# Two attention stages: GpSimd's jobs between the masks, the two turns on TensorE exchanged, a row's sum one place later

## The chip, the cores and the metric

The kernel runs on one core of a Trainium2 chip, in one launch. The time is device microseconds from start to end of one execution. Three executions of the kernel before took 1243.11, 1254.38 and 1258.14 us; their median, 1254.38 us, is the time before.

## The reference

x has 8 rows of 512 tokens of 128 features. Two layers follow each other. Each adds to x an attention and a feed-forward part, both computed from the normalized x:

```python
xn = _layernorm(x)
x = x + _L0_attn_ref(xn, ...) + _L0_ffn_ref(xn, ...)   # amplitude and phase attention; attention over 8 batches, experts (top 1)
xn = _layernorm(x)
x = x + _L1_attn_ref(xn, ...) + _L1_ffn_ref(xn, ...)   # plain attention with biases; experts (top 2)
```

The attention of both layers, which is what the change touches, is causal softmax attention with 16 heads of 8 features over each row of 512 tokens, and a projection by Wo:

```python
scores = where(mask, q @ k.T / sqrt(8), -inf)          # layer 0: of (cos, sin) pairs, scaled for each head
attn = softmax(scores)
out = (attn @ v) @ Wo.T
```

## The kernel before, in words

The program is a list of stages that don't overlap; two of them, `attend0` and `attend1`, are the function `attend` (line 1915) for layer 0 and layer 1. A unit is 4 heads (a group, `GH` = 4) of one row; there are 8 rows of 4 groups, so 32 units. All of a unit's data are f16 stacks of q and k that SyncE loads from HBM into a ring of four places.

Each engine has its own queue, written out by hand as a sequence of steps (`all_steps`, line 164, unrolled). In step t the engines work on several units at once. For unit t, TensorE computes all scores in five chunks c0 to c4 (`maxima`) into a ring of two pairs of PSUM banks, and VectorE reduces each chunk to negated maxima (`reduce`; c1 and c3 in two instructions). For unit t-1 the maxima are split into two f16 parts (`split_maxima`, VectorE), turned by TensorE (`turn_maxima`, one product with 32 columns of weights), copied out of PSUM (`copy_maxima`), and sent by SyncE into two rows of the q tile. For unit t-2 TensorE computes the shifted scores again, transposed, in five chunks and two sides (`probabilities`), with one PSUM bank for each side, ScalarE exponentiates each (`exponentials`) and GpSimd zeroes the upper triangles of the diagonal blocks (`mask`, four for each unit). For unit t-3 TensorE multiplies by the values in four pieces (`mix`: mix 0 behind c1, mix 1 behind c2, mix 2 and 3 behind c3; f32, four heads side by side in column tiles of 32), and ScalarE copies the result to SBUF (`mixT`). For unit t-4 TensorE turns that copy (`turn_mix`, four square f32 transposes) and VectorE divides by the sums (`divide`). Where t-4 is the last group of a row, the step also has `turn_context` (four square transposes, behind c2), a copy by ScalarE, `project` (behind c4), and VectorE's sum of the row (`add_row`).

The three turns and the projection share one PSUM bank, `TURN`, which sets much of the order. In the kernel before, `turn_mix(t-4)` stands behind c0 (line 2233) and `divide` behind the reduction of c0; `turn_maxima(t-1)` stands behind c1 and mix 0 (line 2240), waits for `divide` to have emptied the bank (line 2220), and `copy_maxima` follows the reduction of c1. `add_row(t-4)` is the last thing in VectorE's step (line 2328), before the next step's `split_maxima`; the next `turn_mix` waits for it (line 2216).

GpSimd's queue (lines 2073 to 2093) goes unit by unit: copy the values of unit n into a ring of two (line 2078), start one gather of 128 rows by an indirect DMA in layer 0 or two in layer 1 (line 2086), the four masks of unit n, and in layer 1 two additions for unit n-1 that join the gathered experts' results into `x_sum` (`join_branches`, line 2052). GpSimd's unit n coincides with the step n+2 of the other engines. In layer 0 the gathered rows are used only in a later stage.

## Time and profile before

| | |
|---|---|
| time, median of 3 runs | 1254.38 us (1243.11 to 1258.14) |
| time of the profiled execution | 1254.72 us |
| its span, first to last instruction | 1253.1 us, mean granted clock 0.889 |
| `attend0`, first to last copy of the maxima | 401.6 us to 634.5 us |
| `attend1`, first load of q to the end | 975.7 us to 1253.1 us |

The profile is of one execution. PE is TensorE's matmuls and PEld its weight loads, DVE is VectorE, ACT is ScalarE, POOL is GpSimd; L2171 is line 2171 of the listing. In brackets behind a row of the timeline stands how long the engine had been idle and what ended that. The ends of matmuls are modelled, their starts and those of weight loads are recorded, so pieces of work on TensorE are best measured from weight load to weight load.

### The profile page before, as it was taken

Reading aid. Unit: us, or ns where it says so; the run is one execution under the profiler, and the core shown is the slowest. Engines: PE = TensorE matmul, PEld = TensorE weight load, DVE = VectorE, ACT = ScalarE, POOL = GpSimd, SP = SyncE. Lnnn points to the kernel's source line nnn. Section 1 sums busy time; section 2 is a strip of 40 time slices with the busy share of each in tenths; the row PEclk is TensorE's granted clock in tenths of the full one; section 3 lists DMA queues with packets and bytes.
Section 4 is the critical chain, followed back from the end, with each engine's and each line's share of the span. In section 5 each row is a group of like instructions: output and inputs, shape, how many; then the busy total and the mean of one; then the engine's idle time right before and its main releaser. Section 6 shows DMA issues by size and latency. Waiting matters only on the chain. (4 is left out here: it accounts for less than half of the span.)

```text
span 1253.1 us, 25971 instructions
## 1 busy us (share of the span) xinstructions
PE 996.1 (79%) x8908; PEld 650.2 (52%) x8908; DVE 832.1 (66%) x1875; ACT 680.5 (54%) x1293; POOL 586.7 (47%) x862
## 2 busy tenths in 40 slices
PE   3789753989874999999976463499999699999997
PEld 1456531777672455555533332388888345555542
DVE  1566331799986899999927666133333799999992
ACT  1266443776720777777755353122222377777774
POOL 3467537244432444455433466111110477777774
PEclk9899766899996899999997575699999599999998
DMA  4322032477775222222202233466664111112110
GB/s 135 110 49 54 27 100 89 139 206 201 217 156 132 70 70 70 70 73 77 61 7 63 76 106 96 146 183 192 190 184 136 43 45 53 53 53 53 53 47 27
DMA packets 151525, 122.57 MB, mean 98 GB/s; under 512 B 31712, under 2 KB 134032, under 8 KB 151408
## 3 DMA queue, kind: packets, MB, share of 16 engines
q1 hardware_dynamic: 141664, 102.89, 29.6%
q0 software_dynamic: 8016, 17.71, 4.9%
q8 instruction: 67, 1.10, 0.4%
q10 hardware_dynamic: 1728, 0.46, 0.2%
q14 instruction: 50, 0.41, 0.1%
HBM read 75.75 MB, written 42.61 MB: 94 GB/s over the span
## 5 line engine op out<-in xcount | busy, mean ns | idle before, releaser
L2103 ACT ACTIVATE attend_probs<-attend_attend_ps 128x512 f32<-128x512 f32 x640 | 353.7, 600 | 152.7 <-PE attend_attend_ps L2171 141.5
L2171 PE MATMUL attend_attend_ps<-attend_q,attend_ks 50*128 50x512 f16 (+3 forms) x1024 | 236.6, 307 | 23.1 <-ACT attend_probs L2103 20.3
L2070 POOL TENSOR_SCALAR_AFFINE_SELECT attend_probs<-attend_probs 128x512 f32<-128x512 f32 x256 | 159.6, 636 | 196.7 <-ACT attend_probs L2103 196.1
L2139 PE MATMUL attend_attend_ps<-attend_ks,attend_q 48*128 48x512 f16 (+3 forms) x1024 | 191.5, 317 | 27.8 <-DMA attend_ks<-k_stack 20.2
L2184 PE MATMUL attend_attend_ps<-attend_probs,attend_vals 128*32 128x512 f32 (+3 forms) x2048 | 183.2, 455 | 0.0
L2266 DVE TENSOR_REDUCE attend_neg_max<-attend_attend_ps 128x2 f32<-128x1024 f32 x128 | 155.5, 1215 | 14.3 <-PE attend_attend_ps L2151 9.0
L2151 PE MATMUL attend_attend_ps<-identb,stairs 64*128 64x128 bf16 (+1 forms) x1280 | 144.5, 213 | 0.0
L2171 PEld LDWEIGHTS attend_attend_ps<-attend_q,attend_ks 50*128 50x128 f16 x1024 | 70.4, 94 | 121.6 <-ACT attend_probs L2103 73.7
L2268 DVE TENSOR_REDUCE attend_neg_max<-attend_attend_ps 128x2 f32<-128x768 f32 x128 | 121.9, 952 | 8.2 <-PE attend_attend_ps L2151 7.3
L2151 PEld LDWEIGHTS attend_attend_ps<-identb,stairs 64*128 64x128 bf16 x1280 | 104.4, 100 | 19.3 <-issue 4.7
L1886 PE MATMUL experts_experts_ps<-experts_rowsT,experts_w_in 128*128 128x256 f32 (+1 forms) x468 | 110.2, 386 | 1.6 <-ACT experts_rowsT L1835 1.5
L1851 DVE TENSOR_TENSOR experts_hidden<-experts_experts_ps,experts_gate 128x512 f32<-128x512 f32 x39 | 27.0, 691 | 120.3 <-ACT experts_gate L1827 120.3
L1091 POOL DMA_INDIRECT sorted<-middle_scaled,rank_row x64 | 65.6, 1025 | 59.7 <-issue 39.3
L1814 POOL DMA_DIRECT2D experts_rows<-sorted x39 | 27.7, 711 | 136.7 <-issue 136.7
L1886 PEld LDWEIGHTS experts_experts_ps<-experts_rowsT,experts_w_in 128*128 128x128 f32 (+1 forms) x468 | 82.5, 183 | 17.7 <-ACT experts_rowsT L1835 2.1
L2139 PEld LDWEIGHTS attend_attend_ps<-attend_ks,attend_q 48*128 48x128 f16 x1024 | 68.3, 96 | 41.5 <-DMA attend_ks<-k_stack 20.6
L1827 ACT ACTIVATE experts_gate<-experts_experts_ps 128x512 f32<-128x512 f32 x39 | 23.3, 597 | 121.0 <-PE experts_experts_ps L1886 121.0
L2263 DVE TENSOR_REDUCE attend_neg_max<-attend_attend_ps 128x4 f32<-128x1024 f32 x64 | 78.4, 1225 | 9.6 <-PE attend_attend_ps L2151 9.2
L2086 POOL DMA_INDIRECT attend_moe<-done,back_row x64 | 62.1, 970 | 15.1 <-issue 15.1
L1898 PE MATMUL experts_experts_ps<-experts_w_out,experts_hidden 128*128 128x128 f32 (+1 forms) x468 | 58.7, 275 | 0.9 <-DVE experts_result L1862 0.9
L2184 PEld LDWEIGHTS attend_attend_ps<-attend_probs,attend_vals 128*32 128x32 f32 x2048 | 45.3, 110 | 26.9 <-issue 9.5
L1898 PEld LDWEIGHTS experts_experts_ps<-experts_w_out,experts_hidden 128*128 128x128 f32 (+1 forms) x468 | 55.4, 191 | 1.2 <-issue 1.1
(316 smaller groups left out, 1933.4 us busy)
## 6 DMA issues: line engine op xcount, KB each, us to landing
experts_w_in<-in_L_ffn_w_dram SPq DMA_DIRECT2D x78, 176.0 KB, 2.4
q_stack<-middle_parts SPq DMA_DIRECT2D x24, 256.0 KB
k_stack<-middle_parts SPq DMA_DIRECT2D x24, 256.0 KB
attend_q<-q_stack SPq DMA_DIRECT2D x64, 96.0 KB
attend_ks<-k_stack SPq DMA_DIRECT2D x64, 96.0 KB
middle_w_in<-in_L_ffn_W_dram SPq DMA_DIRECT2D x23, 256.0 KB
middle_w_out<-in_L_ffn_W_dram SPq DMA_DIRECT2D x23, 256.0 KB
experts_rows<-sorted POOLq DMA_DIRECT2D x39, 128.0 KB, 2.5
```

The source lines that it names most:

```text
L1091: pool.indirect_dma_start(k.sorted1, bass.IndirectOffsetOnAxis(ap=k.rank_row[:, c * NT + tile:c * NT + tile + 1], axis=0), scaled[:, c, ti ...
L1886: mm = pe.matmul(ps[0:size[c], hidden_bank(u, bank), half * ROWS:(half + 1) * ROWS], w_in[:, u.phase, w + c * P:w + c * P + size[c]], rows ...
L1898: mm = pe.matmul(ps[:, OUT, a * D:(a + 1) * D], hidden[0:size[c], u.par, c, a * P:(a + 1) * P], w_out[0:size[c], u.phase, c, :], start=(c ...
L2070: pool.affine_select(out=block_, in_=block_, compare_op=ALU.is_ge, fill=0.0, base=0, pattern=[[0, GH], [1, P]], channel_multiplier=-1).the ...
L2103: act.activation(probs[:, u.par, 2 * c + side, :], ps[:, PROB + side, :], ACT.Exp, scale=SCALE ** -2)\
L2139: pe.matmul(ps[:, bank + side, col:col + (qt + 1) * P], q[rows(side, KR), g, pair, qt * P:(qt + 1) * P], ks[rows(side, KR), g, pair, 0:(qt ...
L2151: mm = pe.matmul(span[:, :, col:col + 64], k.stairs[here, stair:stair + P], k.identb[here, here].unsqueeze(1).broadcast_to([64, len(blocks ...
L2171: mm = pe.matmul(ps[:, PROB + side, col:col + S - kt * P], ks[rows(side, KM), g, pair, kt * P:(kt + 1) * P], q[rows(side, KM), g, pair, kt ...
L2184: mm = pe.matmul(ps[32 * h:32 * h + 32, MIX, kt * P:S], vals[:, u.par, kt * GH + h, :], probs[:, u.par, 2 * c + h % 2, col:col + S - kt * ...
L2263: ins = dve.tensor_reduce(out[:, :, :, 1], pair_banks.rearrange("p s (h t) -> p s h t", h=HP), X_AXIS, ALU.max, negate=True)
L2266: ins = dve.tensor_reduce(out[:, :, c // 2, 3], pair_banks, X_AXIS, ALU.max, negate=True)
L2268: dve.tensor_reduce(out[:, :, c // 2, 2], pair_banks[:, :, 0:384], X_AXIS, ALU.max, negate=True)
```

## The change

It touches only `attend`, so both stages, and is a change of order with the waits that belong to it. No arithmetic instruction, DMA or buffer is added or taken away.

1. GpSimd: `copy_values(0)` comes first; then for each unit n: mask 0, the gather (0), in layer 1 the join of branch 0 of unit n-1, masks 1 to 3, the copy of the values of unit n+1, and in layer 1 the second gather and the join of branch 1 of unit n-1. The joins of the last unit stand behind the loop.
2. TensorE: `turn_maxima(t-1)` moves from behind c1 and mix 0 to behind c0; `turn_mix(t-4)` moves from behind c0 to behind c1 and mix 0. The waits for the bank are exchanged: the turn of the maxima waits for the division of unit t-5 and, after a row's end, for the row's sum; the turn of the mix waits for the copy of the maxima of unit t-1.
3. VectorE: `copy_maxima` follows the reduction of c0, `divide` that of c1. `add_row` leaves the end of step t and stands in step t+1 behind `split_maxima`.

```diff
@@ -2049,14 +2049,29 @@
                     pool.wait_ge(k.z_out[i].sem, (TILES[0] + Z_RING - 1 - i) // Z_RING * 16)
             src, at_row = ((k.done0, k.rank_row[:, NT:2 * NT]), (k.done1, k.back_row[:, :]))[layer]
 
-            def join_branches(n):
-
-                for c in range(2):
-                    m = 2 * n + c
-                    pool.wait_ge(gathered[m % 4].sem, (m // 4 + 1) * 16)
-                    if c:
-                        pool.wait_ge(joined.sem, joined.after(n, 0))
-                    pool.tensor_tensor(k.x_sum[:, n, :], k.x_sum[:, n, :], moe[:, c * NT + n, :], ALU.add).then_inc(joined.sem, 1)
+            def copy_values(n):
+                if n >= 2:
+                    pool.wait_ge(mixed.sem, mixed.done(n - 2))
+                b, g = divmod(n, NG)
+                pool.tensor_copy(vals[:, n % 2, :, 0:HD].rearrange("p (j h) d -> p j h d", j=QT),
+                                 k.v_all[:, b, :, g * GH * HD:(g + 1) * GH * HD].rearrange("p j (h d) -> p j h d", h=GH))\
+                    .then_inc(vals_ready.sem, 1)
+
+            def gather(n, c):
+                m = n * (layer + 1) + c
+                if m >= 4:
+                    pool.wait_ge(gathered[m % 4].sem, m // 4 * 16)
+                pool.indirect_dma_start(moe[:, c * NT + n, :], None, src,
+                                        bass.IndirectOffsetOnAxis(ap=at_row[:, c * NT + n:c * NT + n + 1], axis=0))\
+                    .then_inc(gathered[m % 4].sem, 16)
+
+            def join_branch(n, c):
+
+                m = 2 * n + c
+                pool.wait_ge(gathered[m % 4].sem, (m // 4 + 1) * 16)
+                if c:
+                    pool.wait_ge(joined.sem, joined.after(n, 0))
+                pool.tensor_tensor(k.x_sum[:, n, :], k.x_sum[:, n, :], moe[:, c * NT + n, :], ALU.add).then_inc(joined.sem, 1)
 
             def mask(n, i):
 
@@ -2070,27 +2085,25 @@
                 pool.affine_select(out=block_, in_=block_, compare_op=ALU.is_ge, fill=0.0, base=0,
                                    pattern=[[0, GH], [1, P]], channel_multiplier=-1).then_inc(masked.sem, 1)
 
-            for n in range(UNITS + JOIN_AFTER * layer):
-                if n < UNITS:
-                    if n >= 2:
-                        pool.wait_ge(mixed.sem, mixed.done(n - 2))
-                    b, g = divmod(n, NG)
-                    pool.tensor_copy(vals[:, n % 2, :, 0:HD].rearrange("p (j h) d -> p j h d", j=QT),
-                                     k.v_all[:, b, :, g * GH * HD:(g + 1) * GH * HD].rearrange("p j (h d) -> p j h d", h=GH))\
-                        .then_inc(vals_ready.sem, 1)
-
-                    for c in range(layer + 1):
-                        m = n * (layer + 1) + c
-                        if m >= 4:
-                            pool.wait_ge(gathered[m % 4].sem, m // 4 * 16)
-                        pool.indirect_dma_start(moe[:, c * NT + n, :], None, src,
-                                                bass.IndirectOffsetOnAxis(ap=at_row[:, c * NT + n:c * NT + n + 1], axis=0))\
-                            .then_inc(gathered[m % 4].sem, 16)
-                if n < UNITS:
-                    for i in range(QT):
-                        mask(n, i)
+
+            copy_values(0)
+            for n in range(UNITS):
+                mask(n, 0)
+                gather(n, 0)
                 if layer == 1 and n >= JOIN_AFTER:
-                    join_branches(n - JOIN_AFTER)
+                    join_branch(n - JOIN_AFTER, 0)
+                for i in range(1, QT):
+                    mask(n, i)
+                if n + 1 < UNITS:
+                    copy_values(n + 1)
+                if layer == 1:
+                    gather(n, 1)
+                    if n >= JOIN_AFTER:
+                        join_branch(n - JOIN_AFTER, 1)
+            if layer == 1:
+                for n in range(UNITS - JOIN_AFTER, UNITS):
+                    for c in range(2):
+                        join_branch(n, c)
             for i in range(4):
                 pool.wait_ge(gathered[i].sem, UNITS * (layer + 1) // 4 * 16)
 
@@ -2207,19 +2220,17 @@
 
 
 
+            def before_maxima(t):
+                if active(t, 5, UNITS):
+                    pe.wait_ge(context_done.sem, context_done.done(t - 5))
+                    if (t - 5).group == NG - 1:
+                        pe.wait_ge(added.sem, added.done((t - 5).row))
+
             def before_mix(t):
-                if active(t, 2, UNITS):
-                    pe.wait_ge(maxT_ready.sem, maxT_ready.done(t - 2))
-                elif active(t, 5, UNITS):
-                    pe.wait_ge(context_done.sem, context_done.done(t - 5))
-                if active(t, 5, UNITS) and (t - 5).group == NG - 1:
-                    pe.wait_ge(added.sem, added.done((t - 5).row))
-
-            def before_maxima(t):
-                if active(t, 4, UNITS):
-                    pe.wait_ge(context_done.sem, context_done.done(t - 4))
-                elif active(t, 2, UNITS):
-                    pe.wait_ge(maxT_ready.sem, maxT_ready.done(t - 2))
+                if active(t, 1, UNITS):
+                    pe.wait_ge(maxT_ready.sem, maxT_ready.done(t - 1))
+                else:
+                    before_maxima(t)
 
             def step(t):
                 row_ends = active(t, 4, UNITS) and (t - 4).group == NG - 1
@@ -2230,19 +2241,17 @@
                         maxima(t, c)
                     if active(t, 2, UNITS):
                         probabilities(t - 2, c, 1)
-                    if c == 0 and active(t, 4, UNITS):
-                        before_mix(t)
-                        turn_mix(t - 4)
+                    if c == 0 and active(t, 1, UNITS):
+                        before_maxima(t)
+                        turn_maxima(t - 1)
                     if 1 <= c <= 3 and active(t, 3, UNITS):
                         mix(t - 3, c - 1)
                         if c == 3:
                             mix(t - 3, 3)
-                    if c == 1 and active(t, 1, UNITS):
-                        before_maxima(t)
-                        turn_maxima(t - 1)
+                    if c == 1 and active(t, 4, UNITS):
+                        before_mix(t)
+                        turn_mix(t - 4)
                     if c == 2 and row_ends:
-                        if active(t, 1, UNITS):
-                            pe.wait_ge(maxT_ready.sem, maxT_ready.done(t - 1))
                         turn_context(t - 4)
                     if c == 4 and row_ends:
                         project(t - 4)
@@ -2318,15 +2327,15 @@
             def step(t):
                 if active(t, 1, UNITS):
                     split_maxima(t - 1)
+                if active(t, 5, UNITS) and (t - 5).group == NG - 1:
+                    add_row(t - 5)
                 for c in range(MCH):
                     if active(t, 0, UNITS):
                         reduce(t, c)
-                    if c == 0 and active(t, 4, UNITS):
+                    if c == 0 and active(t, 1, UNITS):
+                        copy_maxima(t - 1)
+                    if c == 1 and active(t, 4, UNITS):
                         divide(t - 4)
-                    if c == 1 and active(t, 1, UNITS):
-                        copy_maxima(t - 1)
-                if active(t, 4, UNITS) and (t - 4).group == NG - 1:
-                    add_row(t - 4)
 
             all_steps(UNITS, DEPTH, step, 2 * NG)
 
```

## Rows read from the trace of the kernel before

**Rows 1.** The page, part 1: busy time of each engine, its share of the span, instructions.
```profile
PE 996.1 (79%) x8908; PEld 650.2 (52%) x8908; DVE 832.1 (66%) x1875; ACT 680.5 (54%) x1293; POOL 586.7 (47%) x862
```

**Rows 2.** Windows of four steps, layer 0 and layer 1: busy us (x), granted clock, DMA.
```profile
424.86:454.96 30.10, 27.98 (x376) 15.73 (x368) 28.34 (x51) 23.72 (x47) 14.79 (x24) 1.00 0.26 73
1104.50:1135.80 31.30, 29.09 (x369) 15.79 (x370) 28.94 (x50) 24.15 (x46) 22.19 (x36) 1.00 0.20 53
```

**Rows 3.** Timeline of VectorE (start, us, engine, line): first reciprocal of a row, both layers.
```profile
452.96 0.25 DVE L2295 RECIPROCAL attend_inv<-attend_attend_ps 128x16 f32<-128x16 f32 x1
...
483.06 0.25 DVE L2295 RECIPROCAL attend_inv<-attend_attend_ps 128x16 f32<-128x16 f32 x1
...
1101.14 0.25 DVE L2295 RECIPROCAL attend_inv<-attend_attend_ps 128x16 f32<-128x16 f32 x1
...
1132.47 0.25 DVE L2295 RECIPROCAL attend_inv<-attend_attend_ps 128x16 f32<-128x16 f32 x1
```

**Rows 4.** Timeline, layer 0, from chunk 4 of one step to chunk 1 of the next.
```profile
464.04 0.09 PEld L2171 LDWEIGHTS attend_attend_ps<-attend_q,attend_ks 50*128 50x128 f16 x1 [0.41 <-ACT attend_probs L2103]
...
464.84 1.23 DVE L2263 TENSOR_REDUCE attend_neg_max<-attend_attend_ps 128x4 f32<-128x1024 f32 x1 [0.16 <-PE attend_attend_ps L2151]
...
465.44 0.59 ACT L2122 COPY attend_mixT<-attend_attend_ps 128x512 f32<-128x512 f32 x1
...
466.15 0.42 PEld L2192 LDWEIGHTS attend_attend_ps<-ident,attend_mixT 128*128 128x128 f32 x4 [0.41 <-issue]
...
466.38 0.17 DVE L2281 SCALAR_TENSOR_TENSOR attend_max_parts<-attend_neg_max,attend_max_parts 128x16 f16<-128x16 f32 x1
...
466.74 0.09 PEld L2171 LDWEIGHTS attend_attend_ps<-attend_q,attend_ks 50*128 50x128 f16 x1 [0.17 <-ACT attend_probs L2103]
```

**Rows 5.** Timeline, layer 0, weight loads that open TensorE's pieces, to the next chunk 4.
```profile
467.40 0.16 PEld L2184 LDWEIGHTS attend_attend_ps<-attend_probs,attend_vals 128*32 128x32 f32 x8
468.23 0.09 PEld L2159 LDWEIGHTS attend_attend_ps<-identh,attend_max_parts 128*32 128x32 f16 x1 [0.68 <-DVE attend_context L2299]
...
468.43 0.09 PEld L2171 LDWEIGHTS attend_attend_ps<-attend_q,attend_ks 50*128 50x128 f16 x1
...
469.04 0.16 PEld L2184 LDWEIGHTS attend_attend_ps<-attend_probs,attend_vals 128*32 128x32 f32 x8
469.82 0.09 PEld L2171 LDWEIGHTS attend_attend_ps<-attend_q,attend_ks 50*128 50x128 f16 x1 [0.62 <-ACT attend_probs L2103]
...
471.28 0.09 PEld L2171 LDWEIGHTS attend_attend_ps<-attend_q,attend_ks 50*128 50x128 f16 x1 [0.41 <-ACT attend_probs L2103]
```

**Rows 6.** Timeline, layer 0, where a row ends: a square turn behind a product.
```profile
476.27 0.16 PEld L2184 LDWEIGHTS attend_attend_ps<-attend_probs,attend_vals 128*32 128x32 f32 x8
...
477.06 0.42 PEld L2198 LDWEIGHTS attend_attend_ps<-ident,attend_context 128*128 128x128 f32 x4 [0.62 <-DVE attend_maxT L2288]
...
477.64 0.09 PEld L2171 LDWEIGHTS attend_attend_ps<-attend_q,attend_ks 50*128 50x128 f16 x1 [0.17 <-issue]
```

**Rows 7.** Timeline, layer 0, the row's sum and chunk 1 of the step behind it.
```profile
479.89 1.23 DVE L2263 TENSOR_REDUCE attend_neg_max<-attend_attend_ps 128x4 f32<-128x1024 f32 x1 [0.16 <-PE attend_attend_ps L2151]
...
481.04 0.68 DVE L2312 TENSOR_TENSOR x_sum<-attend_attend_ps,attend_x_tile 128x512 f32<-128x512 f32 x1
...
482.37 0.09 PEld L2171 LDWEIGHTS attend_attend_ps<-attend_q,attend_ks 50*128 50x128 f16 x1 [0.17 <-ACT attend_probs L2103]
```

**Rows 8.** Timeline, layer 1: joins, the split, the turn of the maxima, the second gather.
```profile
1107.72 1.05 POOL L2059 TENSOR_TENSOR x_sum<-x_sum,attend_moe 128x128 f32<-128x128 f32 x2
1107.87 0.33 DVE L2281 SCALAR_TENSOR_TENSOR attend_max_parts<-attend_neg_max,attend_max_parts 128x16 f16<-128x16 f32 x1
...
1109.88 0.09 PEld L2159 LDWEIGHTS attend_attend_ps<-identh,attend_max_parts 128*32 128x32 f16 x1 [0.84 <-DVE attend_context L2299]
...
1110.46 0.95 POOL L2086 DMA_INDIRECT attend_moe<-done,back_row  x1 [0.30 <-issue]
...
1111.28 0.60 ACT L2103 ACTIVATE attend_probs<-attend_attend_ps 128x512 f32<-128x512 f32 x1 [0.19 <-PE attend_attend_ps L2171]
```

## The prediction

> **What bounds the kernel now.** The page's first part comes first: TensorE is busy for 79% of the span, VectorE for 66%, the others less [rows 1]. This is a mean over stages, so I read next the windows of four steps inside each attention: the granted clock is 1.00, TensorE is busy for 27.98 of 30.10 us in layer 0, VectorE for 28.34, ScalarE for 23.72 [rows 2]. Two engines are near their limit, and busy time cannot tell which leads. The row period can be read off VectorE's reciprocals, which come at one place of the order: a row of four steps takes 483.06 - 452.96 = 30.10 us in layer 0 and 1132.47 - 1101.14 = 31.33 us in layer 1 [rows 3]. There are 8 rows in each stage; about 7 of them run in the full pipeline. All that the change does must show in these two numbers.
>
> Then the timeline of one ordinary step, from the weight load that opens chunk 4 to the next one: 464.04 to 471.28, 7.24 us [rows 4, 5]. It falls into two halves.
>
> In the first half TensorE waits. Chunk 4 opens at 464.04, ScalarE's copy of the mix ends at 465.44 + 0.59 = 466.03, the turn of the mix opens at 466.15 behind 0.41 us of idle, and chunk 1 opens at 466.74 [rows 4]. VectorE meanwhile reduces chunk 4 until 464.84 + 1.23 = 466.07, having waited 0.16 for it, and has the split maxima ready at 466.38 + 0.17 = 466.55 [rows 4].
>
> In the second half, from chunk 1 at 466.74 to chunk 4 at 471.28, the pieces follow end to end: mix 0 from 467.40, the turn of the maxima at 468.23, chunk 2 at 468.43, mix 1 at 469.04, chunk 3 at 469.82, then mix 2 and 3 [rows 5]. The releasers in the brackets had finished before: no wait is left in there but that for the division, which ends just as mix 0's columns do. So TensorE's order sets the end in this half, and VectorE follows: its idle 0.16 is a wait for chunk 4's scores.
>
> **The change, part by part.**
>
> Turn of the mix into the full half. Now the slot between mix 0 and chunk 2 holds the turn of the maxima and takes 468.43 - 467.40 = 1.03 us [rows 5]. Afterwards it holds four square f32 transposes. What such a group costs behind a product is shown where a row ends: mix 1 opens at 476.27, the context's turn at 477.06, chunk 3 at 477.64, so the turn takes 0.58; the 0.79 ahead of it are those that mix 1 takes ahead of chunk 3 anyway (469.82 - 469.04 = 0.78) [rows 5, 6]. Mix 0 has 512 columns instead of 384. The turn of the maxima, with weights of the same 32 columns as the mix, opened its load at 0.83; I scale that for the quarter of columns more: 0.78 + 0.83/4 = 0.99 from mix 0 to a square turn. The new slot: 0.99 + 0.58 = 1.57, **0.54 us more** for each step. The low end is 0.83 + 0.58 - 1.03 = 0.38, if the square turn starts as early as the small one.
>
> The row shows that going from the mix to anything but the small turn costs more than the columns. The Trainium skill, TensorEngine Tiling (Array Packing), Tiling Modes, says the same as a rule: changing the tiling mode drains TensorE. By that rule the sum is that of the forecast, without it that of the low end.
>
> Turn of the maxima into the waiting half. It can't open before the split maxima are there, 466.55, nor much after; with 0.05 for the signal and its own slot of 468.43 - 468.23 = 0.20, chunk 1 opens at 466.80 instead of 466.74: **0.06 us more** [rows 4, 5]. The half doesn't shrink, since the turn that left it stood in a wait for ScalarE, and the turn that comes waits for VectorE. That is the core of my argument: TensorE's work leaves idle time and enters full time.
>
> VectorE. The same instructions. The copy of the maxima follows chunk 0, when max_turned is there; the division, one chunk later, must wait for a turn that opens some 1.6 us after chunk 1. It costs nothing more as long as TensorE is late itself, and TensorE is 0.6 later in every step. What is queued behind the division are the reductions of chunks 2 to 4, whose scores are late by as much.
>
> Row's sum. Before, it ran from 481.04 to 481.72 and chunk 1 opened at 482.37 [rows 7]. Chunk 4's reduction ended at 479.89 + 1.23 = 481.12; behind it now come the split, 0.48 as in rows 4, then the sum, 0.68, then the turn of the maxima, 0.25: chunk 1 at 482.53, 0.16 later, where an ordinary step has 0.06. That is 0.1 us a row.
>
> GpSimd. The four masks feed products of the next step; the one that is needed last, mask 3, has until mix 2 and 3. Ahead of masks 1 to 3 now stands a gather of 0.95 and in layer 1 a join of about 0.5 [rows 8], less than a step of 7.24, and the values of unit n+1 are copied two steps ahead of use. Cost nothing. In layer 1 there is a gain: now the joins at 1107.72 run beside the second instruction of the split, which takes 0.33 there and 0.17 in layer 0 [rows 4, 8]. With the copy of the values beside it instead, layer 1 loses these 0.16 us. It also parts the two gathers; in layer 1 an exponential starts, during the second, 0.19 us after the one before it ended [rows 8]. The wait for the division behind 1109.88 and that gap are what layer 1 has over layer 0, 1.23 us a row. I take all of it as gone: both layers then have the same row.
>
> SyncE. The maxima are sent some 1.5 us earlier, the store of a row up to a step's start later; its loads wait for the probabilities as before. Cost nothing. The first gather waits for a mask now, and the last gathers stand a few us ahead of the end of the stage, under the last steps.
>
> **The sum.** Each step grows by 0.54 + 0.06 = 0.60 over layer 0's, a row by 2.4 + 0.1 = 2.5: both layers come to 32.6 us. Over 7 rows layer 0 loses 7 x 2.5 = 17.5 us, layer 1 7 x (32.6 - 31.33) = 8.9 us; together 26.4. Base is the profiled execution, 1254.72 us (span 1253.1), which is the median of the three within 0.4: 1281. Own range of this case: 1271 with the low end (a step 0.16 less, 4 x 0.16 x 14 = 9) to 1290 (the same, more).
>
> **Rivals.**
>
> A. The turn opens early, without emptying the array: 1271 or 1272, by the low end above. For it: the small turn does so. Against it: rows 6.
>
> B. The gathers collide in both layers. The gather of branch 0 stands right behind mask 0 now, just where chunk 2 is exponentiated, and layer 0 would inherit what layer 1 has. Price: between half and all of 1.23 us a row, in 14 rows 9 to 17 us more: 1290 to 1298. For it: the 0.19 us gap [rows 8]. Against: it came with two gathers in a row, and none follow each other now. The Trainium skill, SBUF — State Buffer, Who interferes with whom, has only VectorE and GpSimd share a port, and ScalarE wait for nobody there; by it this case would be empty, but the gap in the row is ScalarE's.
>
> C. The other side: VectorE is the bound, and TensorE's added 0.6 us fits into its idle time. The place is the 0.41 us ahead of chunk 4 and of the turn; it decides if TensorE could run ahead by more than 0.6 there. Then layer 0 stays and layer 1 falls to 30.10 a row, 7 x 1.23 = 8.6 us: 1246; at VectorE's own busy time of about 28.9 a row [rows 2] it would be 1230. For it: VectorE's 28.34 of 30.10. Against it: the 0.16 us that it waits for scores in every step, and the end-to-end chain of rows 5. The Trainium skill, same section, has a VectorE instruction with two SBUF inputs and a GpSimd one that reads SBUF lock each other out. By that rule the joins' new place brings time, 0.16 us a step in layer 1; 0.33 against 0.17 agrees, and the sum has it in already.
>
> D. Waits hide both ways and nothing moves: 1254.
>
> **Chances and range.** Forecast 0.48, A 0.13, B 0.21, C 0.11, D 0.07. Two per cent, about what a measurement of this kernel tells from no change, is 25 us: the line is at 1279.5, close below my forecast. Slower by more: B and 0.6 of the forecast, 0.50. Within 2%: A, D, the rest of the forecast, and nearly all of C, 0.47. Faster by more: 0.03. The range for 8 in 10 runs from 1251 to 1296; it leaves out C and the far end of B.
>
> **What would show it.** In the profile after: from mix 0's weight load to that of chunk 2 about 1.57 us (1.41 for A); from the split's end to chunk 1 0.25; rows of about 32.6 us in both layers; VectorE idle for longer ahead of the reductions of chunks 3 and 4; the second instruction of the split at 0.17 in layer 1. B would show gaps of 0.2 ahead of chunk 2's exponentials in layer 0. A row of 30.1 or less in either layer makes the argument wrong: then TensorE's second half was not full.

## The result, and the profile after

The changed kernel takes 1297.67 us (median of four runs, 1293.87 to 1300.27), the kernel before 1251.57 (four runs, 1243.11 to 1258.14): a ratio of 1.039, interval 1.0348 to 1.0432. It is slower, as forecast, but by 46 us in the medians where 26 were forecast. The profiled execution took 1297.08 us (span 1295.5), against 1254.72 before: 42.4 more.

First the page after, parts 1 and 2 (busy time, and the span in 40 slices; one digit is a tenth):

```profile
PE 1009.2 (78%) x8908; PEld 655.1 (51%) x8908; DVE 841.2 (65%) x1875; ACT 677.4 (52%) x1293; POOL 590.2 (46%) x862
...
PEclk9899766999985999999986655699999599999998
```

The page alone says little: the shares are within two points of [rows 1]. The sums by stage say more. A stage is measured here from its first product on TensorE to its last instruction. The first attention went from 263.9 to 287.7 us, the second from 272.3 to 287.8, all else from 716.9 to 720.0. So 39.3 of the 42.4 us by which the span grew lie in the attentions.

Windows of one row (four steps) after, layer 0 and layer 1, to be held against [rows 2]:

```profile
467.20:499.91 32.71, 28.54 (x370) 15.69 (x370) 29.24 (x50) 23.72 (x45) 14.84 (x24) 1.00 0.24 67
1069.92:1102.63 32.71, 28.57 (x370) 15.64 (x370) 29.24 (x49) 23.72 (x45) 22.56 (x36) 1.00 0.19 51
```

Both layers now have the same row, 32.71 us, 32.6 being forecast. TensorE is busy for 28.5 of them, where it was 27.98 and 29.09: most of what the row gained is idle time. The timeline of TensorE's weight loads, one of its products, and VectorE in one step of layer 1 after, to be held against [rows 4, 5]:

```profile
1079.89 0.96 DVE L2277 TENSOR_REDUCE attend_neg_max<-attend_attend_ps 128x2 f32<-128x768 f32 x1 [0.22 <-PE attend_attend_ps L2164]
...
1080.55 0.09 PEld L2184 LDWEIGHTS attend_attend_ps<-attend_q,attend_ks 50*128 50x128 f16 x1 [0.41 <-ACT attend_probs L2116]
...
1081.35 1.23 DVE L2272 TENSOR_REDUCE attend_neg_max<-attend_attend_ps 128x4 f32<-128x1024 f32 x1 [0.16 <-PE attend_attend_ps L2164]
...
1082.89 0.18 DVE L2290 SCALAR_TENSOR_TENSOR attend_max_parts<-attend_neg_max,attend_max_parts 128x16 f16<-128x16 f32 x1
...
1083.18 0.09 PEld L2172 LDWEIGHTS attend_attend_ps<-identh,attend_max_parts 128*32 128x32 f16 x1 [0.93 <-issue]
...
1083.21 0.22 PE L2172 MATMUL attend_attend_ps<-identh,attend_max_parts 128*32 128x128 f16 x1 [0.69 <-DVE attend_max_parts L2290]
...
1083.36 0.09 PEld L2184 LDWEIGHTS attend_attend_ps<-attend_q,attend_ks 50*128 50x128 f16 x1
...
1084.02 0.16 PEld L2197 LDWEIGHTS attend_attend_ps<-attend_probs,attend_vals 128*32 128x32 f32 x8
...
1085.01 0.42 PEld L2205 LDWEIGHTS attend_attend_ps<-ident,attend_mixT 128*128 128x128 f32 x4 [0.84 <-issue]
...
1085.60 0.09 PEld L2184 LDWEIGHTS attend_attend_ps<-attend_q,attend_ks 50*128 50x128 f16 x1 [0.17 <-issue]
```

From mix 0 (1084.02) to chunk 2 (1085.60) pass 1.58 us, of which the turn of the mix has 0.59: 1.57 was forecast, 1.03 was the slot before [rows 5]. From chunk 4 (1080.55) to chunk 1 (1083.36) pass 2.81, against 2.70 [rows 4]; the turn opens 0.11 behind the split's end at 1083.07, not 0.05. Together 0.55 + 0.11 = 0.66 a step: the plain step went from 7.23 to 7.89. Ahead of the turn of the maxima no weights are loaded for 0.93 us, and by the modelled ends of the products TensorE stands idle for 0.69; what ends that is the split. VectorE waits 0.22 for chunk 3's scores, a wait that it did not have, and 0.16 for chunk 4's as before; the prediction had both waits grow. The split's second instruction takes 0.18 in layer 1, where it took 0.33 [rows 8].

Two lines that speak on the rival of colliding gathers, layer 1 after, ScalarE and GpSimd:

```profile
1077.84 0.97 POOL L2064 DMA_INDIRECT attend_moe<-done,back_row  x1 [0.15 <-issue]
...
1078.13 1.09 ACT L2116 ACTIVATE attend_probs<-attend_attend_ps 128x512 f32<-128x512 f32 x2 [1.16 <-PE attend_attend_ps L2184]
```

Two exponentials run back to back (one group, 1.09 for two of 0.60) beside the gather. The gap of 0.19 of [rows 8] is gone, and none came ahead of chunk 2's exponentials in layer 0.

What the forecast did not have is in three neighbouring windows, layer 1 after (length, busy us of TensorE, weight loads, VectorE, ScalarE, GpSimd, then the granted clock, the DMA's share and GB/s):

```profile
1093.00:1108.60 15.60, 13.68 (x180) 8.11 (x181) 13.59 (x24) 11.02 (x21) 10.25 (x17) 1.00 0.20 56
1108.60:1112.00 3.40, 3.40 (x21) 1.18 (x18) 1.85 (x5) 1.09 (x2) 2.92 (x5) 0.51 0.12 32
1112.00:1127.00 15.00, 12.74 (x174) 6.70 (x170) 13.56 (x23) 11.62 (x22) 9.23 (x16) 1.00 0.15 42
```

For 3.4 us the granted clock is at half, the 1.2 GHz of the two levels. TensorE is "busy" for all of that time because the same matmuls last nearly twice as long (the eight of mix 0 take 1.93 us for 1.07). The weight loads in that stretch, and the division's reciprocal that waits for them:

```profile
1108.94 0.20 PEld L2197 LDWEIGHTS attend_attend_ps<-attend_probs,attend_vals 128*32 128x32 f32 x8 [0.21 <-issue]
...
1110.80 0.72 PEld L2205 LDWEIGHTS attend_attend_ps<-ident,attend_mixT 128*128 128x128 f32 x4 [1.66 <-issue]
...
1111.85 0.10 PEld L2184 LDWEIGHTS attend_attend_ps<-attend_q,attend_ks 50*128 50x128 f16 x1 [0.33 <-issue]
...
1111.96 0.26 DVE L2304 RECIPROCAL attend_inv<-attend_attend_ps 128x16 f32<-128x16 f32 x1 [1.55 <-PE attend_attend_ps L2205]
```

The slot of 1.58 takes 1111.85 - 1108.94 = 2.91 here, and VectorE waits 1.55 for its turn, which it doesn't in a step at full clock. What one such stretch costs is read from the steps: three of the steps with one take 9.42 to 9.47 us instead of 7.89, the fourth, at a row's end, 10.01 instead of 8.48, so 1.55 more on average. The trace after has four while the pipeline is full (up to a stage's last copy of the maxima), at 596.6, 613.7, 1108.6 and 1183.7; the trace before has none there. In both traces the clock also falls while a stage drains (before at 646.5 and 1233.6, for instance), and only the stretches in the full pipeline are counted from here on.

The 42.4 us then add up: rows 7 x (32.71 - 30.09) = 18.3 in layer 0 and 7 x (32.71 - 31.28) = 10.0 in layer 1; four clock stretches, 4 x 1.55 = 6.2; fill and drain of the two stages (the first four steps and what follows the last full one) 4.9; other stages 3.1. The 4.9 is what is left of the attentions' 39.3, not a sum of pieces; the second pair of traces below leaves 7 to 8.

### The profile page after: what moved, and what is told of

The parts are those of the page before. It is cut to its first block and busy times, and to the rows that moved or that the text cites. A ratio compares the mean times of both kernels' runs of the same rounds, so it can differ in the third digit from the quotient of the medians.

```text
span 1295.5 us, 25951 instructions
## 1 busy us (share of the span) xinstructions
PE 1009.2 (78%) x8908; PEld 655.1 (51%) x8908; DVE 841.2 (65%) x1875; ACT 677.4 (52%) x1293; POOL 590.2 (46%) x862
## 5 line engine op out<-in xcount | busy, mean ns | idle before, releaser
L2197 PE MATMUL attend_attend_ps<-attend_probs,attend_vals 128*32 128x512 f32 (+3 forms) x2048 | 186.1, 460 | 2.6 <-ACT attend_mixT L2135 2.6
L2205 PEld LDWEIGHTS attend_attend_ps<-ident,attend_mixT 128*128 128x128 f32 x256 | 29.1, 150 | 59.5 <-issue 32.7
```

The lines of the kernel that those rows point to most:

```text
L2197: mm = pe.matmul(ps[32 * h:32 * h + 32, MIX, kt * P:S], vals[:, u.par, kt * GH + h, :], probs[:, u.par, 2 * c + h % 2, col:col + S - kt * ...
```

## Experiments

The kernel before was run beside each group. In some groups it took about 1220 us and in the others about 1251. The traces say where: from the end of the first attention to the first instruction of the experts pass 111 to 113 us in the former and 133 to 141 in the latter, whatever the kernel. So totals are compared as ratios within a group, and traces by the attentions. "L0" and "L1" are those stages; before, they take 263.9 and 272.3 us. A row's length is given for rows in which the clock holds.

**GpSimd's order alone** on the kernel before.

```diff
-                if n < UNITS: ... copy values; gathers of both branches; masks 0 to 3
-                    join_branches(n - JOIN_AFTER)
+                mask(n, 0); gather(n, 0); join_branch(n - JOIN_AFTER, 0)
+                masks 1 to 3; copy_values(n + 1)
+                gather(n, 1); join_branch(n - JOIN_AFTER, 1)
```

> The kernel before with only GpSimd's new order; TensorE, VectorE and ScalarE keep theirs. My theory, that TensorE's exchanged turns are what costs: here a gain. Layer 0 keeps its row of 30.10 us; layer 1 loses the joins beside the split (second instruction of the split 0.17 instead of 0.33 us) and the second gather beside chunk 2's exponentials, so its row falls from 31.33 towards 30.1 us: 7 to 8 rows x 1.2 = 8 to 10 us less, ratio 0.993. Rival, that the gathers and joins between the masks delay the masks and with them the products: rows longer than 31.33 in layer 1, time 5 to 20 us above the kernel before.

Ratio 0.9971 (0.9950 to 0.9993), L0 263.9, L1 262.6 us. GpSimd, VectorE's split and the reciprocals of a row apart, in layer 1 of this kernel:

```profile
1067.71 0.25 DVE L2308 RECIPROCAL attend_inv<-attend_attend_ps 128x16 f32<-128x16 f32 x1
...
1073.90 0.17 DVE L2294 SCALAR_TENSOR_TENSOR attend_max_parts<-attend_neg_max,attend_max_parts 128x16 f16<-128x16 f32 x1
...
1074.18 0.99 POOL L2064 DMA_INDIRECT attend_moe<-done,back_row  x1 [0.16 <-issue]
...
1075.20 0.47 POOL L2074 TENSOR_TENSOR x_sum<-x_sum,attend_moe 128x128 f32<-128x128 f32 x1
...
1097.80 0.25 DVE L2308 RECIPROCAL attend_inv<-attend_attend_ps 128x16 f32<-128x16 f32 x1
```

The row is 30.09 us, layer 0's own: the 1.23 of excess was GpSimd's place, as the forecast had it, and the stage gives back 9.7 us. This part of the change is a gain, which the other parts bury. But the total fell by 3.5 us only (0.9 to 6.1 by the interval), so a part of the stage's gain does not arrive in it.

**The same kernel once more**, and **the kernel before as its own control**, to find those.

> GpSimd's new order alone once more, since the first comparison gave 0.997 while its trace had layer 1 shorter by 8 to 10 us. Expected: both layers with rows of 30.1 us, 8 to 9 us less in layer 1 than the kernel before, ratio 0.993 to 0.997.

> The kernel before once more, for a trace on the kind of chip on which GpSimd's order alone was run, where the stage between the attentions took 95 us instead of 126. Expected: layer 1's attention 270 to 272 us, 8 us longer than with GpSimd's new order, and the stages outside the attentions some 685 us, which would put the 5 us that are missing in the total outside the attentions. If layer 1 here is only 4 us longer, they were never gained.

The repeat: 0.9973 (0.9947 to 0.9999), L0 262.1, L1 263.4. The control: 0.9991 (0.9939 to 1.0043), L0 263.1, L1 269.6, the rest 715.3. It fell into a group with the long middle stage, while the repeat's rest of 691.0 belongs to the other, so the rests can't be compared. Over all traces layer 1 takes 270.9 us on average in the three of the kernel before and 263.0 in the two with the new order, so the gain is 8 rather than 9.7. It is shown twice; where half of it goes stays open. GpSimd's order alone is still the fastest version run, 0.3% ahead of the kernel before.

**The turns alone**: the changed kernel with GpSimd's order and the row's sum of before.

```diff
-            copy_values(0); for n: mask 0, gather, join, masks 1 to 3, copy, gather, join
+            for n: copy, gathers, masks 0 to 3, join_branches(n - JOIN_AFTER)
-                if active(t, 5, UNITS) and (t - 5).group == NG - 1: add_row(t - 5)
+                (at the step's end) if active(t, 4, UNITS) and (t - 4).group == NG - 1: add_row(t - 4)
```

> The kernel after with GpSimd's order and the place of the row's sum of the kernel before: only the two turns, with the copy of the maxima and the division, are exchanged. My theory: this part alone brings the whole loss. Slot from mix 0 to chunk 2 1.58 us instead of 1.03, step 7.89 in layer 0, row 32.6 to 32.7; in layer 1 the joins beside the split are back and lie on the path (the turn of the maxima now waits for the split itself), so 0.16 a step more than the kernel after: row 33.3. Time 1295 to 1305, ratio 1.037 to 1.045. If it is GpSimd's order or the row's sum that cost, this kernel stays within 1% of the kernel before.

Ratio 1.0505 (1.0467 to 1.0543), more than either theory: L0 292.8, L1 302.2. Yet the rows are shorter than expected, 32.55 us in layer 0 and 33.02 in layer 1, where the plain step is 8.05: the 0.16 of the long split, which lies on the path now. Here too a stretch and its neighbour, in layer 1 (windows as above):

```profile
1061.00:1064.40 3.40, 3.40 (x20) 1.10 (x18) 1.92 (x5) 0.99 (x2) 2.59 (x3) 0.51 0.19 46
1064.40:1072.00 7.60, 6.32 (x88) 3.40 (x85) 6.83 (x12) 5.81 (x11) 3.96 (x7) 1.00 0.10 27
```

There are 16 such stretches, 6 in layer 0 and 10 in layer 1. At 1.55 each they are 25 us, more than the 7 to 16 by which this kernel exceeds its own forecast. So the move of the turns carries the whole loss, and the clock is a part of it.

**The row's sum alone** on the kernel before.

```diff
+                if active(t, 5, UNITS) and (t - 5).group == NG - 1:
+                    add_row(t - 5)      # behind split_maxima(t - 1)
...
-                if active(t, 4, UNITS) and (t - 4).group == NG - 1:
-                    add_row(t - 4)      # at the step's end
```

> The kernel before with only the row's sum moved behind the split of the next step. The turn of the mix then waits for a sum that ends about 0.4 us later, once a row: 7 rows x 2 layers x 0.4 = 5 us more at most, ratio 1.00 to 1.005, and nothing if the division, not the turn, is what the step waits for. Rival, that the row's sum brings a good part of the 46 us: ratio above 1.01.

Ratio 1.0043 (1.0022 to 1.0063); row 30.59 in layer 0 (+0.50), 31.12 in layer 1, no stretch at half clock. A small loss, as expected, and all of it in layer 0; layer 1's row is 0.16 shorter than before. The joins still run beside the split in this kernel, and its timeline in layer 1 shows the split long, just where the previous kernel with the new GpSimd order has 0.17:

```profile
1076.51 0.17 DVE L2279 TENSOR_SCALAR attend_max_parts<-attend_neg_max 128x16 f16<-128x16 f32 x1
1076.71 0.35 DVE L2281 SCALAR_TENSOR_TENSOR attend_max_parts<-attend_neg_max,attend_max_parts 128x16 f16<-128x16 f32 x1
1076.98 0.68 DVE L2316 TENSOR_TENSOR x_sum<-attend_attend_ps,x_sum 128x512 f32<-128x512 f32 x1
```

The two gathers still follow each other as well, and yet no exponential of layer 1 is late by the 0.19 to 0.22 us of [rows 8]. Here a pair runs back to back beside the second gather:

```profile
1071.37 0.95 POOL L2086 DMA_INDIRECT attend_moe<-done,back_row  x1 [0.30 <-issue]
...
1071.37 1.09 ACT L2103 ACTIVATE attend_probs<-attend_attend_ps 128x512 f32<-128x512 f32 x2 [0.73 <-PE attend_attend_ps L2171]
```

So two gathers in a row alone don't make the exponentials late. The plain step of layer 1 is 7.35 here, 0.12 over layer 0's with the long split alone, where it was 7.45 to 7.56 before.

**The row's sum put back** in the changed kernel.

```diff
-                if active(t, 5, UNITS) and (t - 5).group == NG - 1: add_row(t - 5)
+                (at the step's end) if active(t, 4, UNITS) and (t - 4).group == NG - 1: add_row(t - 4)
```

> The kernel after with the row's sum back at its old place, ahead of the split: the turns exchanged and GpSimd's new order. With the turns alone layer 0 had a row of 33.03 us and 6 stretches at the lower clock, layer 1 a row of 34.8 and 10; the kernel after has 32.71 and 2 in each. If the row's sum behind the split is what helps once the turns are exchanged (the split is ready 0.7 us sooner behind a row's end, though the turn waits for the sum as well), layer 0 here is as with the turns alone, 33.0 and some 6 stretches, and layer 1 equals it, since GpSimd's order has taken the joins away: ratio 1.045. If it is GpSimd's order that thins out the stretches, both layers are at 32.7 to 33.0 with 2 or 3: ratio 1.038.

Ratio 1.0321 (1.0288 to 1.0354); L0 290.3 with four stretches at half clock, L1 283.7 with one; the row is 32.55 in both. The two attentions take 574.0 us, against 575.5 and 572.7 in two traces of the changed kernel, but that has the stretches in it. In rows, the changed kernel's 32.71 is 0.16 longer, all of it in the step behind a row's end (8.45 for 8.29): the sum behind the split costs 14 x 0.16 = 2.2 us there. Between this kernel and the turns alone only GpSimd's order differs, and the stretches fall from 16 to 5, in layer 1 from 10 to 1, in layer 0 from 6 to 4 (one trace each).

**ScalarE's copy of the mix ahead of chunk 4's exponentials**, on the kernel before: it asks whether the wait ahead of the turn of the mix could have been shortened there instead.

```diff
-                if active(t, 3, UNITS):      # behind the loop over c
+                    if c == 3 and active(t, 3, UNITS):      # inside it
                         ... act.copy(mixT[:, :], ps[:, MIX, :])
```

> The kernel before with ScalarE's copy of the mix moved from behind chunk 4's exponentials to ahead of them. If the first half of the step is a wait for that copy, as I read it, the turn of the mix opens up to 0.15 us sooner behind chunk 4 (2.11 us before) and a step of layer 0 takes 7.10 to 7.15 instead of 7.24: 4 to 8 us less, ratio 0.995. Rival: chunk 4's exponential, now 0.2 us later, holds up the next chunk 0, and the step gets 0.1 longer: ratio 1.005.

Ratio 1.0038 (1.0012 to 1.0065), step 7.36 instead of 7.23 in layer 0. The rival was right: TensorE's idle ahead of the next chunk 0, which waits for the exponentials of chunk 4 behind the copy, is 0.63 instead of 0.44 us.

**Both kernels again**, for the run-to-run spread of stages and stretches.

> The kernel before itself, for its trace on the chip on which the parts are run; nothing changed. Expected: rows of 30.1 us in layer 0 and 31 to 31.3 in layer 1, no stretch of TensorE's lower clock inside the attentions; the stages outside the attentions some 30 us shorter than in the first profile, as in the profiles of the parts. If the attentions differ too, the comparison of parts by their stages needs that control.

> The kernel after itself, on the same chip as its variants. Expected: rows of 32.7 us in both layers, a few stretches at the lower clock (4 in the first profile), each in a step that is about 1.5 us longer; ratio 1.035 to 1.045.

Before against itself: 0.9992 (0.9943 to 1.0041), L0 261.0, L1 270.7, no stretch at half clock. After: 1.0349 (1.0267 to 1.0432), L0 285.9, L1 286.8, rows of 32.71 again, three stretches, at 600.8, 1078.6 and 1235.7. So the stretches are the changed kernel's own, but their places aren't fixed. The rest of before, all outside the attentions, was 720.5, not shorter as expected. That makes the 3.1 us outside the attentions part of the spread: the five traces of the two kernels with the long middle stage have rests of 715.3 to 720.5.

**Eight small products in the idle ahead of the turn of the maxima**, in the changed kernel; they compute nothing that is used.

```diff
+                        for _ in range(8):
+                            pe.matmul(ps[0:32, TURN, 0:P], k.identh[:, 0:32], k.identh[:, :], start=True, stop=True)
                         turn_maxima(t - 1)
```

> The kernel after with eight small products (32 x 128 f16 identities, about 0.05 us each) put ahead of the turn of the maxima, in the half of the step in which TensorE waits for VectorE. They write a part of the bank that the turn overwrites; the output doesn't depend on them. Theory: that half has some 0.9 us of idle, so 0.45 us of work is free there: steps stay at 7.89 us, rows at 32.7. And if it is the idle time that lets the clock fall, the stretches at the lower clock go: 5 to 7 us less than the kernel after. Rival: TensorE's time is on the path there too, steps of 8.3 us, 25 us more.

Ratio 1.0371 (1.0276 to 1.0467); L0 286.0, L1 287.8; no stretch at half clock in either layer. Weight loads of TensorE around them, layer 1:

```profile
1069.90 0.45 PEld L2248 LDWEIGHTS attend_attend_ps<-identh 128*32 128x32 f16 x8 [0.19 <-issue]
1070.57 0.09 PEld L2173 LDWEIGHTS attend_attend_ps<-identh,attend_max_parts 128*32 128x32 f16 x1 [0.22 <-DVE attend_max_parts L2293]
1070.73 0.09 PEld L2185 LDWEIGHTS attend_attend_ps<-attend_q,attend_ks 50*128 50x128 f16 x1
```

The step even shrinks, 7.81 for 7.89: the turn's own slot is 0.16 instead of 0.18, and its releaser is shown as the split. But behind a row's end the products stood after the wait for the row's sum, which opened late, and that step grew from 8.45 to 8.94: row 32.96. These 14 x 0.49 = 6.9 us eat what the stretches gave back, and the 5 to 7 us that were expected don't show.

**The same, but not in the step behind a row's end.**

```diff
+                        row_waits = active(t, 5, UNITS) and (t - 5).group == NG - 1
+                        for _ in range(0 if row_waits else 8): ... the same product
```

> The kernel after with the eight small products only in the steps that don't wait for a row's sum. In the run with them in every step, the ordinary steps took 7.81 us instead of 7.89 and no stretch at the lower clock was left, but the step behind a row's end grew from 8.45 to 8.94, since there the products started only after the sum. Expected: that step back at 8.4 to 8.5, rows of 32.5, and, if the idle time of the ordinary steps is what lets the clock fall, no stretch or at most one: 4 to 8 us less than the kernel after, ratio about 1.03. If the idle time behind the row's sum is what counts, the stretches are back, three or four, and the time is that of the kernel after.

Ratio 1.0298 (1.0267 to 1.0328); L0 284.4, L1 282.7; row 32.47; again no stretch. The attentions take 567.1 us, 8.4 and 5.6 less than in the two traces of the changed kernel. These have four and three stretches, 6.2 and 4.7 us, and rows longer by 0.24, 14 x 0.24 = 3.4: 9.6 and 8.1 in all. The totals alone would not show it: the ratio's interval lies below the changed kernel's first one (1.0348 to 1.0432) and inside its second (1.0267 to 1.0432). Windows over 190 us of layer 1, of before, after and this kernel, in this order, one fence each:

```profile
1040.00:1230.00 190.00, 176.32 (x2223) 94.61 (x2219) 172.22 (x293) 147.08 (x274) 134.19 (x218) 1.00 0.19 51
```

```profile
1040.00:1230.00 190.00, 165.86 (x2098) 90.05 (x2095) 166.99 (x281) 135.14 (x258) 129.73 (x207) 0.98 0.18 49
```

```profile
1040.00:1230.00 190.00, 176.74 (x2281) 99.29 (x2276) 169.22 (x286) 138.93 (x264) 131.86 (x212) 1.00 0.18 50
```

TensorE is busy for 0.93 of the first and the third, which hold their clock, and for 0.87 of the second, which doesn't. The products in the idle took the stretches away in two kernels and four stages; that the idle brings them is shown by this, how much idle it takes is not.

**The same eight products in the full half**, between mix 0 and the turn of the mix: if TensorE's order sets the end there, they must cost their own length.

```diff
+                        for _ in range(8): ... the same product
                         turn_mix(t - 4)
```

> The kernel after with the same eight small products put between mix 0 and the turn of the mix, in the half that I read as full. Theory: each of them lies on the path: step 7.89 + 8 x 0.053 = 8.31 us, rows of 34.4, 58 steps x 0.43 = 25 us more than the kernel after. Rival, that the step's length is set by VectorE or by the waits in the other half: no change to the kernel after.

Ratio 1.0548 (1.0447 to 1.0649); step 8.32, row 34.42, where 8.31 and 34.4 were expected. L0 297.3, L1 303.3: 27.9 more than the second trace of the changed kernel, 25 being expected. Four stretches in layer 1, none in layer 0. The loads there:

```profile
1074.11 0.16 PEld L2198 LDWEIGHTS attend_attend_ps<-attend_probs,attend_vals 128*32 128x32 f32 x8
1074.58 0.09 PEld L2255 LDWEIGHTS attend_attend_ps<-identh 128*32 128x32 f16 x1 [0.31 <-DVE attend_maxT L2300]
1074.99 0.43 PEld L2255 LDWEIGHTS attend_attend_ps<-identh 128*32 128x32 f16 x7 [0.33 <-issue]
1075.53 0.42 PEld L2206 LDWEIGHTS attend_attend_ps<-ident,attend_mixT 128*128 128x128 f32 x4
1076.12 0.09 PEld L2185 LDWEIGHTS attend_attend_ps<-attend_q,attend_ks 50*128 50x128 f16 x1 [0.17 <-issue]
```

TensorE's timeline has the eight products themselves in one group:

```profile
1074.99 0.61 PE L2255 MATMUL attend_attend_ps<-identh 128*32 128x128 f16 x8
```

The slot is 1076.12 - 1074.11 = 2.01 for 1.58. Equal work costs 0.43 a step in one half and nothing in the other: that is the claim of two halves, shown on the chip.

## Why the prediction was right, and where it was wrong

**Where the bound lies: right.** TensorE's second half was full and its first half waited. The fill in both halves shows it, and the row of 32.71 in both layers excludes the case in which VectorE was the bound.

**The turn of the mix: right, with some luck in the price.** 1.58 for 1.57, and 0.99 us from mix 0 to the turn as forecast; the 1.41 of case A did not come. But both were built on the small turn's load 0.83 behind mix 0, and that load came when it did because the division ended 0.05 before it, as its bracket says [rows 5]. With small products there and the division out of the way, the first load comes at 0.47 and the product still at 0.88 (1074.99 - 1074.11). The small turn's product came at 0.88 too (468.28 - 467.40), the square turn's at 0.99, so the square turn costs 0.11 of waiting. The Trainium skill, TensorEngine Tiling (Array Packing), Tiling Modes, has a change of the tiling mode drain TensorE. These 0.11 agree. The small turn's product in the trace before:

```profile
468.28 0.22 PE L2159 MATMUL attend_attend_ps<-identh,attend_max_parts 128*32 128x128 f16 x1
```

**The turn of the maxima: 0.11 for 0.06**, since the turn follows the split by 0.11. In 56 steps these 0.05 are 3 us. The prediction's 0.05 for the signal was short.

**The row's sum: size off, small.** Of chunk 4's reduction behind a row's end and what follows it, in layer 1 after:

```profile
1097.72 1.23 DVE L2272 TENSOR_REDUCE attend_neg_max<-attend_attend_ps 128x4 f32<-128x1024 f32 x1 [0.16 <-PE attend_attend_ps L2164]
...
1099.36 0.68 DVE L2325 TENSOR_TENSOR x_sum<-attend_attend_ps,x_sum 128x512 f32<-128x512 f32 x1
...
1100.11 0.09 PEld L2172 LDWEIGHTS attend_attend_ps<-identh,attend_max_parts 128*32 128x32 f16 x1 [0.89 <-issue]
...
1100.29 0.09 PEld L2184 LDWEIGHTS attend_attend_ps<-attend_q,attend_ks 50*128 50x128 f16 x1
```

From the reduction's end, 1098.95, to chunk 1 pass 1.34 us; before they were 482.37 - 481.12 = 1.25 [rows 7]. That is 0.09 more where 0.16 was forecast, and no more than the 0.11 of an ordinary step. The forecast added up two things that the parts show apart: exchanging the turns makes the step behind a row's end cheaper (0.40 over a plain step, from 0.58), and the sum's new place gives 0.16 of that back. On the kernel before the same move costs 0.5 a row in layer 0. So the row came out at 32.71 for 32.6 because two small errors partly cancel.

**GpSimd: right.** Layer 1's excess is gone, in the change and alone. How much of the 1.23 is the split was left open. With the row's sum alone the long split is there and the late exponentials are not, and layer 1's plain step is 0.12 over layer 0's, of the 0.22 to 0.33 before. The rest goes with the late exponentials. That the two gathers in a row cause them, as the prediction took it, is not borne out by that kernel, which has them too. The Trainium skill, SBUF — State Buffer, Who interferes with whom, has VectorE with two inputs in SBUF and GpSimd's reads lock each other out: 0.35 beside the joins and 0.17 without them agree. The same section of the Trainium skill has ScalarE wait for nobody. [rows 8] show its exponential late, and no run says by what.

**The rival of colliding gathers: its time came nearest, its mechanism did not occur.** The kernel landed at 1297.67, at the far end of that case's 1290 to 1298, without one exponential late as in [rows 8]. A time inside a rival's bounds is no proof of the rival.

**The sum: wrong.** The step that failed is "Over 7 rows layer 0 loses 7 x 2.5 = 17.5 us, layer 1 7 x (32.6 - 31.33) = 8.9 us; together 26.4". The two terms measured 18.3 and 10.0, so they are 1.9 us short. What is missing stands beside them, put at nothing: the clock, 6.2 us, and the filling and draining steps, 4.9, which also hold turns; 3.1 more lie in other stages, inside their spread. The prediction read a granted clock of 1.00 in the windows before and carried it over without asking what held it up. Yet its own argument moved work out of TensorE's idle time, so it had to leave one longer idle in each step, 0.69 us as it came out, in an engine that had been busy for 0.93 of the stage. With 1254.72 + 28.3 + 6.2 + 4.9 = 1294 the time would have been within 4 us.

**Left open.** Why the turns alone have 16 stretches and the change four. In layer 1 TensorE's products stand idle for 0.85 us ahead of the turn of the maxima in the former and 0.69 in the latter, and there are 10 and 2; but in layer 0 it is 0.69 in both, and there are 6 and 2. Nor does the longest single idle decide: with the row's sum alone on the kernel before, TensorE is idle for 0.96 us in one piece once a row in layer 1, and has no stretch. The share doesn't tell it either: TensorE is busy for 165.73 of the 190 us of layer 1 in the turns alone, 165.86 after, though matmuls at half clock count nearly double in it. What sets off a stretch isn't shown. Also open is where some 4 to 5 us of the gain of GpSimd's order go, and why layer 1's exponentials came late.

## What to carry to other kernels

Split the step into the part where TensorE waits and the part where it is full, and ask of each moved piece which part it leaves and which it enters; the price of a piece is its slot there, load to load, with what the engine needs to change shape, not its busy time. When a change leaves TensorE more idle, add a term for its clock, and look for it in short windows, since a mean of 0.98 hides it. Take the bracket of a weight load for what it is: a time between loads, ended by whatever stands there, and no property of the array. Take an edit of several parts apart: here one of three was a gain of 8 us in its stage, and the whole lost 42.

## What the runs showed of the hardware

- The granted clock fell to half for 3.4 us at a time in the full pipeline of kernels whose TensorE was busy for 0.87 to 0.88 of the stage (after 4 and 3 stretches, the turns alone 16, the row's sum put back 5, the fill in the full half 4, all in layer 1 and none in layer 0 at the same share), and in none of those at 0.91 to 0.93 (before, its variants, both fills in the waiting half). The share does not say how often. A stretch lengthened its step by 1.55 us, about a fifth.
- With small products that compute nothing in the waiting half the clock held, and they made the step 0.08 us shorter: the turn behind them opened 0.06 after the split, not 0.11.
- Behind mix 0, the weights of a small product of the same 32 columns went in after 0.47 us and its product started at 0.88 (1074.58 and 1074.99 against 1074.11); of a square turn both came at 0.99.
- A split beside GpSimd's joins takes 0.33 to 0.35 us, without them 0.17 to 0.18, and costs its plain step 0.12 to 0.16 us. Exponentials that came 0.2 us late beside two gathers in a row came on time once these were parted, but also in a kernel that left the gathers in a row.
